# Reordered masks on POOL, a shared turned copy on DVE, and V read once a pass, in a fused two-branch layer kernel on one core

## What is computed

```
x = x + 0.5 * ffn(layernorm(x))
x = x + attn(layernorm(x))
x = x + 0.5 * ffn(layernorm(x))
```

```
q, k     = x Wq, x Wk                        # per head
mix      = one_hot(top2(x Ws)) * sigmoid(top2 value)
v        = sum over experts of mix * (x Wv)
attn     = softmax(q k^T / 8) v
mask     = one_hot(top2(x Wd))               # per head, 8 experts
res      = sum over heads, experts of mask * attn * Wo
```

## Time and profile before

| what | kernel before |
|---|---|
| median of 3 runs (range) | 2421.73 us (2420.21 to 2424.61) |
| profiled execution, its own time | 2416.01 us |
| its span, first to last instruction | 2414.2 us |
| TensorE's granted clock, mean | 0.998 |
| busy: PE, weight loads | 96%, 89% |
| busy: DVE, ACT, POOL | 84%, 84%, 48% |
| DMA engines, mean busy share of q1 | 54.9% |

### The profile page before, as it was taken

The page is one execution under the profiler, slowest core; times in us unless marked ns, Lnnn a source line. Parts: engine busy times, 40 slices in busy tenths (PEclk is TensorE's granted clock), DMA queues, the critical chain, the costliest instruction groups (busy, mean ns, idle before and its releaser), DMA issues.

```text
span 2414.2 us, 120555 instructions
## 1 busy us (share of the span) xinstructions
PE 2316.1 (96%) x49920; PEld 2149.1 (89%) x49920; DVE 2032.5 (84%) x3626; ACT 2020.9 (84%) x6245; POOL 1157.8 (48%) x1126
## 2 busy tenths in 40 slices
PE   3999999999999999999999999999999999999997
PEld 3988888989899999999989999999999999999987
DVE  5888878888888888888888888888888888888874
ACT  3988787888888888888888888888888888888885
POOL 3454545455354454454454454554554554544431
PEclk9999999999999999999999999999999999999999
DMA  4555455655556556556556556555556555555563
GB/s 125 165 162 155 142 153 146 167 159 166 164 156 178 164 158 177 160 156 175 162 163 173 160 161 172 160 162 162 175 157 168 167 163 163 164 164 163 167 171 105
DMA packets 660701, 388.23 MB, mean 161 GB/s; under 512 B 232512, under 2 KB 585664, under 8 KB 660160
## 3 DMA queue, kind: packets, MB, share of 16 engines
q1 hardware_dynamic: 659728, 379.67, 54.9%
q10 hardware_dynamic: 432, 0.85, 0.1%
HBM read 191.64 MB, written 188.74 MB: 158 GB/s over the span
## 4 chain that ended last, share of the span: by engine, by line
PE 83%; ACT 6%; DVE 6%; issue 3%; POOL 1%; DMA 0%; SPq 0%; DVEq 0%; ACTq 0%; POOLq 0%
PE psT L471 18%; PE psS L426 15%; PE psT L488 7%; PE psS L514 7%; PE psT L439 6%; PE psT L514 6%; PE psT L490 6%; PE psT L489 5%; ACT PB L785 5%; PE psT L483 5%; PE psT L453 4%; DVE NMAX L665 2%; DVE QK L729 1%; PE psT L520 1%; PE psT L572 1%
## 5 line engine op out<-in xcount | busy, mean ns | idle before, releaser
L785 ACT ACTIVATE PB<-psS,NMAX 128x256 f32<-128x256 f32 x2048 | 947.3, 497 | 100.8 <-DVE NMAX L665 99.9
L471 PE MATMUL psT<-V,PT 128*64 128x64 f32 x16384 | 541.3, 224 | 9.9 <-issue 9.4
L471 PEld LDWEIGHTS psT<-V,PT 128*64 128x64 f32 x16384 | 503.2, 138 | 37.8 <-issue 12.4
L785 ACT ACTIVATION_READ_ACCUMULATOR PB<-psS,NMAX 128x1 f32 x2048 | 471.2, 230 | 0.0
L426 PE MATMUL psS<-QK 64*128 64x256 f32 x6144 | 464.0, 290 | 1.2 <-DVE PT L736 1.2
L729 DVE TENSOR_TENSOR QK<-psT,QK 128x512 fp32r<-128x512 f32 x512 | 340.5, 687 | 144.1 <-ACT QK L794 142.2
L426 PEld LDWEIGHTS psS<-QK 64*128 64x128 f32 x6144 | 398.4, 187 | 22.9 <-issue 21.6
L665 DVE TENSOR_REDUCE NMAX<-psS 128x2 f32<-128x512 f32 x512 | 329.0, 684 | 83.5 <-PE psS L426 80.2
L794 ACT ACTIVATE QK<-psT 128x512 fp32r<-128x512 f32 x512 | 299.5, 630 | 84.8 <-PE psT L490 70.7
L891 POOL TENSOR_TENSOR BT<-MT,diagv 128x1024 f32<-128x1024 f32 x128 | 304.9, 2382 | 108.1 <-DMA MT<-MIXd 108.1
L667 DVE TENSOR_REDUCE NMAX<-psS 128x4 f32<-128x1024 f32 x256 | 310.8, 1214 | 0.0
(11 more groups left out here) (120 smaller groups left out, 4776.4 us busy)
## 6 DMA issues: line engine op xcount, KB each, us to landing
Vd<-VM SPq DMA_DIRECT2D x512, 128.0 KB, 2.3
V<-Vd SPq DMA_DIRECT2D x512, 128.0 KB, 3.2
AOd<-AO SPq DMA_DIRECT2D x256, 256.0 KB, 2.5
AR<-AOd SPq DMA_DIRECT2D x256, 256.0 KB, 4.1
PJd<-PJ SPq DMA_DIRECT2D x64, 512.0 KB, 2.8
PR<-PJd SPq DMA_DIRECT2D x256, 128.0 KB, 2.6
MIXd<-MIX SPq DMA_DIRECT2D x64, 128.0 KB, 2.3
MT<-MIXd SPq DMA_DIRECT2D x64, 128.0 KB, 3.2
```

Of the source, the lines that this page charges most:

```text
L471: last = eng.matmul(M[64 * u:64 * u + 64, (t * NT + it) * DH:(t * NT + it + 1) * DH], PT[:, t, jt, cols], V[:, pm % 2, 4 * r + t, jt, :], ...
L785: eng.activation(PB[:, ab, j, it, :], psS[:, ab, j, it, :], ACT.Exp, bias=NMAX[:, ab, j, it:it + 1], accum_out=SUM[:, p % 2, it, 4 * r + t ...
```

## The change

On POOL the first `spread_mask` moves ahead of x's normalisation, and the second waits until GM of pass p+2 is done. On DVE F1 moves behind AO's copy (r 1), `largest` of GS ahead of it (r 0), and the turned bank 3 is copied in r 0, 1 and 3, in r 1 ahead of GM; ACT then copies three banks in these quarters. On the SP queue V is read once a pass, in r 0, over all 128 rows, once both halves are stored; in r 3 a wait for product n-1 stands ahead of PR's reads; and PJ's store moves behind V's and AO's stores in r 2.

```diff
--- before.py
+++ after.py
@@ -317,13 +317,13 @@
                     own = slice(8 // PARTS * i, 8 // PARTS * (i + 1))
                     eng.dma_start(stored[:, own, :], mixed[:, own, :]).then_inc(s_vw[half], 16)
 
-            def load_values(q, half):
-                rows = slice(64 * half, 64 * half + 64)
+            def load_values(q):
                 eng.wait_ge(s_split, 4)
-                eng.wait_ge(s_vw[half], 16 * PARTS * (q + 1))
+                for half in range(2):
+                    eng.wait_ge(s_vw[half], 16 * PARTS * (q + 1))
                 wait_full(eng, "product", 4 * (q - 2) + 3)
-                loaded = V[rows, q % 2].rearrange("p h n d -> p (h n d)")
-                stored = Vd[q % 2].rearrange("(p x) -> p x", p=P)[rows]
+                loaded = V[:, q % 2].rearrange("p h n d -> p (h n d)")
+                stored = Vd[q % 2].rearrange("(p x) -> p x", p=P)
                 for i in range(PARTS):
                     own = slice(H * NT * DH // PARTS * i, H * NT * DH // PARTS * (i + 1))
                     eng.dma_start(loaded[:, own], stored[:, own]).then_inc(s_value[q % 2], 16)
@@ -331,7 +331,7 @@
             for n in QUARTERS:
                 p, r = divmod(n, 4)
                 if r == 0 and runs(p):
-                    load_values(p, 1)
+                    load_values(p)
                 if r == 0 and runs(p + 1):
                     q = p + 1
                     eng.wait_ge(s_mixw, 16 * (q + 1))
@@ -356,18 +356,10 @@
                     wait_freed(eng, "output", p - 2, 0)
                     wait_freed(eng, "output", p - 2, 1)
                     eng.dma_start(x_rows(out, s), X[:, s % XRING].rearrange("p n c -> p (n c)")).then_inc(s_out[s % XRING], 16)
-                if r == 2 and runs(p + 2):
-                    q = p + 2
-                    wait_freed(eng, "expert", q, 0)
-                    wait_freed(eng, "expert", q, 1)
-                    if q >= 2:
-                        eng.wait_ge(s_pr, 16 * PARTS * (q - 1))
-                    eng.dma_start(PJd[q % 2].rearrange("(p x) -> p x", p=P),
-                                  PJ[:, :, :, :].rearrange("p e n d -> p (e n d)")).then_inc(s_pjw, 16)
                 if r == 2 and runs(p + 1):
                     store_values(p + 1, 0)
-                if r == 3 and runs(p + 1):
-                    load_values(p + 1, 0)
+                if r == 3:
+                    wait_full(eng, "product", n - 1)
                 if r == 3 and runs(p + 2):
                     q = p + 2
                     eng.wait_ge(s_pjw, 16 * (q + 1))
@@ -385,6 +377,14 @@
                     if m >= 8:
                         eng.wait_ge(s_ar, 16 * PARTS * (m // 4 - 1))
                     eng.dma_start(AOd[m // 4 % 2].rearrange("(p r x) -> p r x", p=P, r=4)[:, m % 4, :], AO[:, m % 2, :]).then_inc(s_aow[m % 2], 16)
+                if r == 2 and runs(p + 2):
+                    q = p + 2
+                    wait_freed(eng, "expert", q, 0)
+                    wait_freed(eng, "expert", q, 1)
+                    if q >= 2:
+                        eng.wait_ge(s_pr, 16 * PARTS * (q - 1))
+                    eng.dma_start(PJd[q % 2].rearrange("(p x) -> p x", p=P),
+                                  PJ[:, :, :, :].rearrange("p e n d -> p (e n d)")).then_inc(s_pjw, 16)
                 if r == 0 and runs(p - 1):
                     q = p - 1
                     eng.wait_ge(s_maskw, 16 * (q + 1))
@@ -458,7 +458,7 @@
                 pm, r = divmod(m, 4)
                 wait_vacant(eng, "product", m)
                 if r == 0:
-                    eng.wait_ge(s_value[pm % 2], 32 * PARTS * (pm // 2 + 1))
+                    eng.wait_ge(s_value[pm % 2], 16 * PARTS * (pm // 2 + 1))
                 M = bank("product", m)
                 for t in (2, 3, 0, 1):
                     if t % 2 == 0:
@@ -683,9 +683,6 @@
                     statistics(s_stat, 4 * (p + 3), 0, x_of(p + 3))
                 if r == 1 and runs(q):
                     highest(at + 3)
-                    if q >= 1:
-                        eng.wait_ge(s_share, SHARES * (q - 1) + 3)
-                    first(F1[:, :, :], at + 4)
                 if r == 2 and runs(q):
                     eng.wait_ge(s_pick, at + 6)
                     largest(1, GM[:, :, :])
@@ -698,15 +695,20 @@
                     eng.tensor_scalar(SG[:, :, :], SG[:, :, :], 1.0, None, ALU.add).then_inc(s_pick)
                     eng.wait_ge(s_pick, at + 12)
                     eng.reciprocal(SG[:, :, :], SG[:, :, :]).then_inc(s_pick)
+                if r == 0 and runs(q):
+                    wait_freed(eng, "gates", q)
+                    largest(0, GS[:, :, :])
                 if works(n - 1):
                     m = n - 1
                     wait_full(eng, "product", m)
                     if m >= 2:
                         eng.wait_ge(s_aow[m % 2], 16 * (m // 2))
                     eng.tensor_copy(AO[:, m % 2, :], bank("product", m)).then_inc(freed("product", m))
+                if r == 1 and runs(q):
+                    if q >= 1:
+                        eng.wait_ge(s_share, SHARES * (q - 1) + 3)
+                    first(F1[:, :, :], at + 4)
                 if r == 0 and runs(q):
-                    wait_freed(eng, "gates", q)
-                    largest(0, GS[:, :, :])
                     equal(0, GS[:, :, :], at + 1)
                 if r == 1 and attends(p - 2):
                     wait_freed(eng, "output", p - 2, 0)
@@ -727,13 +729,13 @@
                         m = 2 * n + 2 + ab
                         eng.wait_ge(s_qhi, m + 1)
                         eng.tensor_tensor(QK[:, 1, ab], bank("qk", m).rearrange("p (k t) -> p k t", k=2), QK[:, 0, ab].bitcast(F32), ALU.subtract).then_inc(freed("qk", m))
+                if works(n) and r != 2:
+                    wait_turned(eng, n, 3)
+                    wait_full(eng, "product", n - 1)
+                    eng.tensor_copy(turned_rows(3), turned(n, 3).rearrange("p (k x) -> p k x", x=64)).then_inc(was_copied(n, 3))
                 if r == 1 and runs(q):
                     eng.wait_ge(s_pick, at + 5)
                     eng.scalar_tensor_tensor(GM[:, :, :], F1[:, :, :], LOWEST, GS[:, :, :], ALU.mult, ALU.add).then_inc(s_pick)
-                if works(n) and r in (0, 3):
-                    wait_turned(eng, n, 3)
-                    wait_full(eng, "product", n - 1)
-                    eng.tensor_copy(turned_rows(3), turned(n, 3).rearrange("p (k x) -> p k x", x=64)).then_inc(was_copied(n, 3))
                 if r == 0 and attends(p - 3):
                     M = bank("attn_state", p - 3)
                     wait_full(eng, "attn_state", p - 3)
@@ -867,7 +869,7 @@
                         wait_full(eng, "attn_w", attn_pass[nth[q] - 1])
                     eng.activation(AAT[:, :], bank("attn_turn", q)[:, 0:T], ACT.Identity, bias=lnb[:, 0:1], scale=lng[:, 0:1]).then_inc(freed("attn_turn", q))
                 if works(n):
-                    for t in (2, 0, 1) if r in (0, 3) else (2, 3, 0, 1):
+                    for t in (2, 3, 0, 1) if r == 2 else (2, 0, 1):
                         wait_turned(eng, n, t)
                         wait_full(eng, "product", n - 1)
                         eng.activation(turned_rows(t), turned(n, t).rearrange("p (k x) -> p k x", x=64), ACT.Copy).then_inc(was_copied(n, t))
@@ -943,11 +945,14 @@
                     eng.tensor_tensor(xs, xs, bo[:, :].unsqueeze(1).to_broadcast([P, NT, C]), ALU.add).then_inc(s_xa)
                 if r == 1 and runs(p + 1):
                     spread_mix(p + 1, 0)
+                if r == 1 and runs(p - 1):
+                    spread_mask(p - 1, 0)
                 if r == 1 and runs(p + 3):
                     wait_full(eng, "xturn", p + 2)
                     normalise(s_stat, 4 * (p + 3), s_rstd, s_xn, 0, XN, x_of(p + 3))
                 if r == 1 and runs(p - 1):
-                    spread_mask(p - 1, 0)
+                    if runs(p + 2):
+                        eng.wait_ge(s_pick, PICKS * (p + 2) + 6)
                     spread_mask(p - 1, 1)
                 if r == 1 and attends(p - 2):
                     a = nth[p - 2]
```

## The result

The changed kernel takes 2479.65 us (median of 4 runs, 2474.99 to 2494.87) against 2423.17 us for the kernel before beside it: a ratio of 1.0238, 95% interval 1.0212 to 1.0265, so 56 us slower. The forecast was 2438 us with 2464 as its upper end: the direction was right, and of the 56 us the forecast had 16. The profiled execution took 2482.3 us, span 2480.5, at a mean granted clock of 0.994 of full speed (0.998 before). The clock plays no part: the r 0 quarters are as long as before to within 0.1 us over 25 passes.

A forecast was written before the change was run, and what follows sets the result against it. TensorE, 83% of the chain of waits, was taken to bound the kernel; -12 - 6 + 25 + 12 = +19 us on the 2421.7 us median gave 2441, taken as 2438 us, range 2402 to 2464.

The forecast's parts named there:

- Part 1: Scores of r 2: DVE copying bank 3 in r 1 removes PE's mid-scores idle in 58 of 116 waits, -12 us.
- Part 2: GM on DVE in r 1: without POOL's masks beside it, it takes about 0.7 us; worth 0 on the path.
- Part 3: SP queue: emptying r 3 removes most product pauses, -6 us; MT, MASKR's store and MASKT's read come 1.3 us later.
- Part 4: Odd passes: late MT delays POOL's BT into DVE's S0, +1.0 us in each of 25 passes, +25 us.
- past the window: Rival, odd passes: MT over 2.3 us later, BT starts behind S0, ST and FW; -11 us, 2411; chance 0.10.
- slower still: Rival: MT 2 us late in the window, MASKT in every even pass ahead of F1; +64 us, 2486; chance 0.10.
- Part 5: Even passes: POOL's first mask, waiting for MASKT, holds DVE's F1; 0.7 us in two of three, +12 us.

The follow-up runs named there:

- e1: The changed kernel with the SP queue of the kernel before (V in two halves, no wait, PJ's store early), POOL, DVE and ACT as changed: 2406.4 us.
- e11: e1 with POOL's order of before (x's normalisation, then both masks, no wait for GM), the copy still ahead of GM: 2418.7 us.
- e6: The kernel before with only DVE's copy of bank 3 in r 1 added, placed behind GM: 2483.7 us.
- e7: The changed kernel with POOL's order of before in r 1: x's normalisation, then both masks, no wait for GM: 2452.1 us.
- e2: The kernel before with one edit, V read whole once a pass in r 0: 2432.1 us.
- e3: The kernel before with one edit, the wait for product n-1 ahead of PR's reads in r 3: 2446.7 us.
- e14: e1 with only MT's read moved, behind the stores of the mask and of AO in r 0: 2464.8 us.
- e10: e1 with PJ's store at its late place in r 2: 2413.7 us.
- e8: The changed kernel without the wait for the product in r 3: 2424.8 us.
- e4: The changed kernel with V read in two halves again, the wait and PJ's later store kept: 2447.8 us.
- e9: e1 with V read whole in r 0, behind MT's read: 2471.7 us.
- e5: The changed kernel with MT's read issued ahead of the whole read of V in r 0: 65 us against the changed kernel.
- e13: e1 with V read whole in r 0 and MT's read issued between V's second and third part: 2412.4 us.

## Why the prediction was wrong in size

**Part 1, the third copy (-12), held, with its condition.** The idle in the scores went, 116 times to 69 in e1 as in the changed kernel (58 was forecast); r 2 shrank by 4.3 + 8.0 us over passes 10 to 59 of e1. Its sentence that DVE has the time only if GM gets shorter proved the strongest of the text: ahead of a long GM the copy wins nothing (e11), and behind it, a place that the change doesn't use, it costs 65 us (e6).

**Part 2, GM alone (0), held for GM's length** (681 ns at the median) and failed in its last sentence, "The second mask comes no later than now, because now it queues behind the normalisation and the first mask." It compared the two masks' places in the queue and left out when MASKT arrives, and what is queued behind: the wait now stands ahead of x's normalisation too, and in r 2 PE waits for what ends POOL's row, AXN (22.4 us, 17 times) and in five passes the second mask (2.7 us). **This is the step that failed most:** +46.5 us in r 2 of even passes, of which POOL's old order gives back 33 (e7).

**Part 3, the queue.** The -6 for product pauses is right for V's removal from r 3 (e2: 12.4 to 4.8 us) and wrong for the whole part, because the wait adds pauses (21.9 us in e3, 34.4 in the changed kernel, waits for V included). Its guess at what they are, instructions of PE that come late, is borne out, see below. The delay of 1.3 us for MT and MASKT was mis-sized: the landings moved by 2.5 to 3.7 us and 2.4 to 3.6 us. The issue moved by 1.2 to 1.8 us, and that alone filled the estimate of "1.0 to 2.0 us" for both; what was missing is the transfer, 4.8 us from issue to landing at the median instead of 3.2, since 1 MB of V is ahead of it. I had put V's other half megabyte into the sentence and nothing into the sum. That V lands before its product asks for it was wrong too, in 6 of 25 even passes.

**Part 4, BT against S0 (+25), the mechanism held exactly, and the shift overshot.** The threshold, BT's start at 7.3 us, and the slope of about one are what the first curve shows (7 to 7.5: nothing; 8 to 8.5: +0.8), and so is the far edge at 9.9 us. With 2.5 to 3.7 us in place of 1.3, passes p % 4 = 1 lay in the window (+17.3) and passes p % 4 = 3 beyond it (-6.7): forecast and the "past the window" rival each came true for half of the odd passes, and part 4 came to +11. The sign that was to show it, S0's median near 1.5 us, didn't come (284 ns). e14 shows what a shift of 2 us into the window costs: 58 us. The "slower still" rival had the right size, +64, for the wrong place.

**Part 5, the first mask against F1 (+12), measured +4.3.** Pass 28 has it (F1 2.39 us, r 1 10.3), and passes 10 and 40; in the others MASKT came too late for the collision, and made r 2 pay. The other 3.3 of the +7.6 us in r 1 of the even passes are the product's waits for V, for which the prediction had no term.

**PJ's store** was not priced by me, and may hold some 7 us (e10).

**The sum as measured**, over passes 10 to 59: r 2 of the even passes +46.5, r 1 of the even passes +7.6, r 1 of the odd ones +10.6, r 2 of the odd ones -4.5, all r 3 -3.0, together +57; the other passes and the start bring it to +66 between the two profiled executions, 56 by the medians. The copy's gain is inside these figures. So the forecast lacked one term, r 2 of the even passes, that is most of the loss. All other places bring +11 in these passes and +20 over the whole run, where the forecast had +19 for everything: near it in sum, from terms that were off one by one. e1, the engines' edits without the queue's, is faster than both kernels, 2406.4 us.

**What the pauses named "issue" are.** They have no semaphore behind them, but the trace also holds PE's own instructions as they are fetched, as transfers of 16 KB. From part 3 of the page of after (queue and kind: packets, MB, share of 16 engines):

```profile
q8 instruction: 400, 6.55, 1.2%
```

PE's program has 102401 instructions, so a packet carries 256 of them. In passes 10 to 59 of all 16 traces the two products (plain and masked) hold 237 pauses over 0.3 us that are no wait for V or for a mask. All of them stand at the same place of such a block of 256 instructions, to within one, and all end 1.2 to 1.7 us after a 16 KB instruction packet has landed. So in these pauses PE waits for its next block of instructions. They sum to 8.1 us before, 8.3 in e1, 1.9 in e2, 1.3 in e8, 14.2 in e3, 17.7 in e4 and 27.3 in the changed kernel: few where V's read is gone from r 3 and the queue doesn't wait, most with the wait. They aren't added to the loss in full, since PE would often have waited for POOL's row instead (pass 30). What stays open is why a packet comes later with the wait; no run separated that.

## What to carry to other kernels

When an operation that waits for a transfer is moved ahead of others on its engine, price everything that is then behind the wait, and who waits for that, at the landing time that the transfer will have after the change. A transfer's lateness costs by windows, not by a slope: the same 2 us were free, worth 58 us, or free again, depending on which operation of the other engine was running when it landed. And two edits that are worth nothing or less alone (shorter GM, one more copy) can be worth 17 us together, so undo them in pairs before dropping one.

## What the runs showed of the hardware

- POOL and DVE hold each other wherever both read two tensors of SBUF: a POOL product of 1.96 or 2.39 us stretches DVE's EQ from 0.68 to 2.62 us, F1 from 0.69 to 2.39, FW from 0.41 to 2.58 and S0 from 0.28 to 2.38, each about until POOL's product ends. In pass 25 of e9 EQ and BT end 0.56 us apart. The one that starts first is not the one that is stretched: BT keeps 2.36 to 2.39 us in nearly all of these. Where DVE starts first it is POOL's operation that grows: beside a running F1, which keeps its 0.68 us, the mask product takes up to 2.48 us instead of 1.96 (changed kernel). This agrees with what the Trainium skill (SBUF - State Buffer, SBUF: two separate sides) says, that the pair of ports which DVE and POOL share is locked for a whole instruction and the loser is blocked until its end: FW, 0.41 us alone, ended 0.29 us after BT in pass 25 of the changed kernel, from its timeline:

```profile
1014.79 2.39 POOL L893 TENSOR_TENSOR BT<-MT,diagv 128x1024 f32<-128x1024 f32 x1 [5.54 <-DMA MT<-MIXd]
1014.90 2.57 DVE L630 TENSOR_TENSOR FW<-EQ,rampb 128x512 bf16<-128x512 bf16 x1
```

- A small read behind 1 MB of others in the same queue lands 5.1 us after its issue, behind half as much 3.2, and in front of them 2.4 (MT in e2, before, and e5).
- The same transfers in another order can cost 65 us (MT's read ahead of V's instead of behind it, e5 against the changed kernel) or 59 us (MT's read in front of V's four parts instead of in their middle, e9 against e13), with no engine's work changed.
- PE can stand still for its own instructions: up to 2.35 us at a block of 256 of them in the changed kernel (pass 32, r 2), each time until 1.2 to 1.7 us after the block's 16 KB packet landed.
